# Four of a visit's eight source one-hots gathered from an identity table in DRAM

## The reference

```python
def gcn_conv(x, W, b, src, dst, n_nodes):
    h = x @ W
    deg = jax.ops.segment_sum(jnp.ones_like(dst, dtype=h.dtype), dst, num_segments=n_nodes)
    dinv = jnp.where(deg > 0, jax.lax.rsqrt(deg), 0.0)
    norm = dinv[src] * dinv[dst]
    msgs = h[src] * norm[:, None]
    out = jax.ops.segment_sum(msgs, dst, num_segments=n_nodes)
    return out + b
...
src, dst = add_self_loops(edge_index, n)
h = gcn_conv(x, W1, b1, src, dst, n)
h = jax.nn.relu(h)
out = gcn_conv(h, W2, b2, src, dst, n)
```

## Time and profile before

| | us |
|---|---|
| median of three runs | 4810.34 |
| lowest and highest | 4807.37, 4814.28 |
| the profiled execution, whole | 4806.03 |
| its span | 4803.5 |
| busy in the span: TensorE, VectorE, ScalarE, GpSimd | 3900.7, 2679.1, 1793.9, 1492.7 |

### The profile page before, as it was taken

One profiled execution on the slowest core, in us unless ns is written; L12 is line 12 of the kernel. 1 busy time (PEld: TensorE's weight loads), 2 busy tenths in 40 slices (PEclk: granted clock), 3 DMA queues, 4 the chain that ended last, 5 costly groups with the idle time before them and its releaser, 6 DMA issues. The chain is left out here.

```text
span 4803.5 us, 77604 instructions
## 1 busy us (share of the span) xinstructions
PE 3900.7 (81%) x19093; PEld 2693.1 (56%) x19094; DVE 2679.1 (56%) x8404; ACT 1793.9 (37%) x4836; POOL 1492.7 (31%) x1513
## 2 busy tenths in 40 slices
PE   6989996599975888885877809859588996599999
PEld 4566664344433466664555504325587776488887
DVE  4489999677785367767777786000897213011010
ACT  0067775377761022221666623001896101111111
POOL 0155553477750155553777700000000000211110
PEclk9999998699997999997999959979899996799999
DMA  3278884388862378775888810180000001634342
GB/s 108 78 253 270 271 268 154 109 273 272 270 205 82 86 257 260 255 257 178 277 262 262 266 42 8 40 309 0 0 0 16 8 24 66 258 116 165 104 156 91
DMA packets 204806, 765.45 MB, mean 159 GB/s; under 512 B 36862, under 2 KB 60270, under 8 KB 204734
## 3 DMA queue, kind: packets, MB, share of 16 engines
q0 software_dynamic: 119328, 566.15, 36.8%
q1 hardware_dynamic: 82334, 194.49, 11.6%
q10 hardware_dynamic: 3072, 3.94, 0.3%
HBM read 838.08 MB, written 26.53 MB: 180 GB/s over the span
## 5 line engine op out<-in xcount | busy, mean ns | idle before, releaser
L689 PE MATMUL l_psZ<-X,ident 128*128 128x396 f32 (+3 forms) x2656 | 811.5, 428 | 0.4 <-issue 0.3
L887 POOL DMA_INDIRECT a_g<-fs,pair_src x664 | 716.5, 1079 | 304.2 <-issue 162.0
L625 POOL DMA_INDIRECT X<-fs,near_src x664 | 627.9, 946 | 481.8 <-DVE l_zr L657 167.1
L963 PE MATMUL a_psO<-a_g,a_sel 128*128 128x396 f32 (+1 forms) x1992 | 726.2, 509 | 43.7 <-DVE a_g L911 31.2
L689 PEld LDWEIGHTS l_psZ<-X,ident 128*128 128x128 f32 x2656 | 498.5, 191 | 189.4 <-issue 5.9
L942 ACT ACTIVATE a_g<-a_g,L 128x99 f32<-128x99 f32 (+1 forms) x1494 | 529.1, 428 | 182.4 <-DMA a_g<-fs,pair_src 169.2
L686 PE MATMUL l_psZ<-fd,l_spread 128*128 x1328 | 449.4, 418 | 150.4 <-DVE l_zr L659 69.2
L963 PEld LDWEIGHTS a_psO<-a_g,a_sel 128*128 128x128 f32 x1992 | 376.2, 195 | 314.8 <-issue 120.4
L919 DVE TENSOR_TENSOR acc<-acc,a_psO 128x386 f32 (+2 forms) x664 | 342.9, 558 | 238.3 <-PE a_psO L963 180.3
L686 PEld LDWEIGHTS l_psZ<-fd,l_spread 128*128 128x128 f32 x1328 | 235.1, 190 | 230.4 <-issue 210.3
L2117 PEld LDWEIGHTS r_psH<-r_rowsT,r_w 128*128 128x128 f32 x2916 | 331.2, 193 | 17.4 <-DMA r_w<-in_L_ffn_w 10.5
(11 more groups left out here) (393 smaller groups left out, 5437.0 us busy)
## 6 DMA issues: line engine op xcount, KB each, us to landing
r_w<-in_L_ffn_w SPq DMA_DIRECT2D x54, 3456.0 KB
l_dsts<-near_rows SPq DMA_DIRECT2D x166, 128.0 KB
hw_w<-in_L_ffn_w SPq DMA_DIRECT2D x8, 2304.0 KB
disp<-in_L_ffn_w SPq DMA_DIRECT2D x8, 2304.0 KB
X<-fs,near_src POOLq DMA_INDIRECT x664
a_g<-fs,pair_src POOLq DMA_INDIRECT x664
H<-in_L_ffn_b SPq DMA_DIRECT2D x27, 384.0 KB
X<-in_x SPq DMA_DIRECT2D x2, 3456.0 KB
```

Of the source, the lines that this page charges most:

```text
L625: nc.gpsimd.indirect_dma_start(out=g[:, n % RING, :], out_offset=None, in_=fs, in_offset=bass.IndirectOffsetOnAxis(ap=R.near_src[:, n:n + ...
L689: last = nc.tensor.matmul(psZ[k][:, a, 0:hi - lo], R.ident[:], g[:, j, lo:hi], start=False, stop=True, skip_group_check=True)
L887: nc.gpsimd.indirect_dma_start(out=g[:, n % RING, 0:width], out_offset=None, in_=table, in_offset=bass.IndirectOffsetOnAxis(ap=R.pair_src[ ...
L963: last = nc.tensor.matmul(psO[j][:, a, 0:hi - lo], sel[:, j, k, :].bitcast(F32), g[:, j * 2 + k, lo:hi], start=(k == 0), stop=(k == 1))
```

## The change

`setup` makes an identity table `eye` of 1280 rows by 1280 columns in bfloat16 in DRAM. VectorE clears a strip of 128 by 2432, ScalarE puts the 128 by 128 identity into it and issues ten transfers of 128 rows, each a window of the strip that is shifted by a block; ScalarE waits for the source list before it issues them and for all ten at the end. The same one-hot products that list the sources of the pairs also list the sources of the last four tiles of each visit: `R.wide_src`, 196 columns of indices, by eight small VectorE instructions, eight matmuls and two copies.

In `edge_counts` GpSimd issues 196 gathers, four per visit, each of 128 rows of `eye` with 2560 bytes, into a buffer `fetched` that holds four visits; from the fifth visit on it waits for the matmuls of the visit four before. VectorE makes three source one-hots per visit instead of six and ScalarE one instead of two. TensorE also waits for the gathered rows of the visit; its loop now holds four visits instead of two.

`R.high` is now allocated after `edge_counts`, so its cast moves from `norm_counted` to `gcn_layers`: ScalarE casts a block of H and then copies that block of the counts. VectorE's `low` of a block waits for the cast. In `norm_counted` ScalarE zeroes seven blocks before the square root and three behind it.

```diff
+FETCHED, FETCHES = 4, 4
...
+        @block.scalar
+        def _(act):
+            act.wait_ge(s_strip, 1)
+            act.wait_ge(s_id, 1)
+            nc.scalar.copy(strip[:, ROWS - P:ROWS], R.ident[:]).then_inc(s_strip, 1)
+            act.wait_ge(s_strip, 2)
+            act.wait_ge(s_src, 48)
+            for b in range(NB):
+                act.dma_start(R.eye[b * P:(b + 1) * P, :], strip[:, (NB - 1 - b) * P:(NB - 1 - b) * P + ROWS]).then_inc(s_eye, 16)
+            act.wait_ge(s_eye, 16 * NB)
...
+            nc.vector.memset(strip[:], 0.0).then_inc(s_strip, 1)
...
+            for k in range(FETCHED):
+                last = nc.vector.tensor_scalar(wide_tile[:, k, :], wide_u, float(WIDE), float(WIDE - FETCHED + k), ALU.mult, ALU.add)
+            chain(last)
+            for q in range(4):
+                last = nc.vector.tensor_scalar(wide_hot[:, q], wide_tile[0:TQ], tile_nof[:, q:q + 1], None, ALU.is_equal)
+            last.then_inc(s_hot, 1)
...
+            for h, k0, k1 in ((0, 0, 2), (1, 2, FETCHED)):
+                nc.vector.tensor_copy(R.wide_src[:, k0 * WIDE_VISITS:k1 * WIDE_VISITS], fetched[h])
...
+            pe.wait_ge(s_hot, 3)
+            for h, k0, k1 in ((0, 0, 2), (1, 2, FETCHED)):
+                for q in range(4):
+                    nc.tensor.matmul(fetched[h], rowsf[:, 0, q, :], wide_hot[:, q, k0:k1].rearrange("t k v -> t (k v)"), start=(q == 0), stop=(q == 3))
...
-            for b in range(NB // 2):
+            for b in range(NB - 3):
                 empty(b)
             square_roots(nc, act, W, W.val, W.root)
-            for b in range(NB):
-                act.wait_ge(s_row, b + 1)
-                nc.scalar.copy(R.high[:, b, :], R.H[:, b, :])
-            for b in range(NB // 2, NB):
+            for b in range(NB - 3, NB):
                 empty(b)
...
-    BY_ACT = 2
+    BY_ACT = 1
+    MADE = WIDE - FETCHED
...
-        pick = c.sb("pick", [P, 2, WIDE, ROWS], BF16)
+        pick = c.sb("pick", [P, 2, MADE, ROWS], BF16)
+        fetched = c.sb("fetched", [P, FETCHES, FETCHED, ROWS], BF16)
...
+            for v in range(WIDE_VISITS):
+                if v >= FETCHES:
+                    pool.wait_ge(s_mm, v - FETCHES + 1 + 2)
+                for k in range(FETCHED):
+                    nc.gpsimd.indirect_dma_start(
+                        out=fetched[:, v % FETCHES, k, :], out_offset=None, in_=R.eye,
+                        in_offset=bass.IndirectOffsetOnAxis(ap=R.wide_src[:, k * WIDE_VISITS + v:k * WIDE_VISITS + v + 1], axis=0)).then_inc(s_fetched[v % FETCHES], 16)
...
-                for k in range(WIDE - BY_ACT):
+                for k in range(MADE - BY_ACT):
...
-            def multiply(i, s):
-                v = i * 2 + s
+            def multiply(i, f):
+                v, s = i * FETCHES + f, f % 2
...
+                pe.wait_ge(s_fetched[f], i * 16 * FETCHED + 16 * FETCHED)
                 for b in range(NB):
                     for k in range(WIDE):
-                        last = nc.tensor.matmul(psC[s][:, b * P:(b + 1) * P], pick[:, s, k, b * P:(b + 1) * P], sel[:, s, k, :],
-                                                start=(k == 0), stop=(k == WIDE - 1))
+                        own = pick[:, s, k, b * P:(b + 1) * P] if k < MADE else fetched[:, f, k - MADE, b * P:(b + 1) * P]
+                        last = nc.tensor.matmul(psC[s][:, b * P:(b + 1) * P], own, sel[:, s, k, :], start=(k == 0), stop=(k == WIDE - 1))
...
             for b in range(NB):
+                nc.scalar.copy(R.high[:, b, :], R.H[:, b, :]).then_inc(s_high, 1)
                 nc.scalar.activation(counts[:, b, :], R.CT[:, b, :], ACT.Copy, accum_out=degree[:, b:b + 1]).then_inc(s_count, 1)
...
             for b in range(NB):
+                dve.wait_ge(s_high, b + 1)
                 low_part(b, R.H)
```

More of the change, by code:

```diff
@@ L1435, in edge_counts @@
         away = c.sb("away", [P, BY_ACT, ROWS], F16)
-        pick = c.sb("pick", [P, 2, WIDE, ROWS], BF16)
+        pick = c.sb("pick", [P, 2, MADE, ROWS], BF16)
+        fetched = c.sb("fetched", [P, FETCHES, FETCHED, ROWS], BF16)
+        s_fetched = [c.sem(f"fetched{f}") for f in range(FETCHES)]
         sel = c.sb("sel", [P, 2, WIDE, P], BF16)
@@ L1471, in make @@
                     act.wait_ge(s_away, v * BY_ACT + n + 1)
-                    last = nc.scalar.activation(pick[:, s, WIDE - BY_ACT + n, :], away[:, n, :], ACT.Relu, scale=-1.0, bias=one[:])
+                    last = nc.scalar.activation(pick[:, s, MADE - BY_ACT + n, :], away[:, n, :], ACT.Relu, scale=-1.0, bias=one[:])
                 last.then_inc(s_pick, 1)
@@ L1528, in multiply @@
                 pe.wait_ge(s_pick, v + 2)
+                pe.wait_ge(s_fetched[f], i * 16 * FETCHED + 16 * FETCHED)
                 for b in range(NB):
                     for k in range(WIDE):
-                        last = nc.tensor.matmul(psC[s][:, b * P:(b + 1) * P], pick[:, s, k, b * P:(b + 1) * P], sel[:, s, k, :],
-                                                start=(k == 0), stop=(k == WIDE - 1))
+                        own = pick[:, s, k, b * P:(b + 1) * P] if k < MADE else fetched[:, f, k - MADE, b * P:(b + 1) * P]
+                        last = nc.tensor.matmul(psC[s][:, b * P:(b + 1) * P], own, sel[:, s, k, :], start=(k == 0), stop=(k == WIDE - 1))
                 last.then_inc(s_mm, 1)
-            visits(pe, multiply)
+            with pe.Fori(0, WIDE_VISITS // FETCHES) as i:
+                for f in range(FETCHES):
+                    multiply(i, f)
+            for f in range(WIDE_VISITS % FETCHES):
+                multiply(WIDE_VISITS // FETCHES, f)
 def gcn_layers(nc, R, name, layers):
@@ L2144, in program @@
         R.X = sb("X", [P, NB, D])
-        h_at = nc.sbuf_base
+        h_at = -(-nc.sbuf_base // 32) * 32
         R.H = sb("H", [P, NB, D])
```

17 lines of the change are left out of this document (11 added, 6 removed).

## The result

The changed kernel takes 4874.88 us (median of four runs, 4869.28 to 4877.04) against 4811.51 for the kernel before (4807.37 to 4814.28): 1.0128 times as long, with a 95% interval of 1.0116 to 1.0141. That is **+63 us**, where +20.5 was forecast and the range ended at +42.

The account below looks back on a forecast made before the run. In `edge_counts` three engines were within a microsecond, VectorE's one-hots last; the change would make GpSimd's gathers the bound. 26.5 - 10.0 + 0.8 + 3.2 = +20.5 us, giving 4831 us; range 4796 to 4852.

Parts of the forecast that it names:

- `setup`: Setup stage: +3.2 us, TensorE last there with eight more products and two copies; lists and table transfers hidden.
- `norm_counted`: Normalization stage: 10.0 us earlier, as the casts leave and two zeroings move ahead; VectorE then last.
- `edge_counts`: Edge count stage: +26.5 us, GpSimd's four gathers and their delays making a visit 6.1 us, 0.5 more than before.
- `gcn_layers`: Graph layers: +0.8 us, TensorE starting behind one returned cast; flags some 20 us in, without cover up to 3 more.
- under the source one-hots: Edge counts: gathers starting beside VectorE's source one-hots wait, 0.5 us a visit, the middle between 0 and 0.9.
- 6.1: Edge counts: us per visit, from 5.0 for four gathers, 0.6 under `sel` and 0.5 under the source one-hots.
- only `sel` holds them up: Rival, edge counts: gathers delayed by `sel` alone, 5.5 to 5.6 us a visit, total 4801 to 4806; chance 0.16.
- The other half of the same step: Edge counts: one-hots wait for gathers in turn, 0.2 us up to some 0.6, some of 0.7 us or more.
- Wrong in kind would be a stage in which GpSimd waits for TensorE: Sign, edge counts: GpSimd waiting for TensorE (the buffer) would show the forecast wrong in kind; no size given.

Follow-up runs that it names:

- A: Occasions (chips 4, 3 and 0, and the first measurement) on which the kernel before took 4813.42, 4810.97 and 4807.68 us, as in the first measurement.
- B: Two occasions (chips 2 and 5) on which the kernel before took 4578.14 and 4576.11 us.
- a1: The changed kernel itself, run again in B; 0.9978 of the kernel before.
- n1: The change with VectorE's `sel` run only twice at the start of the stage (counts left out); 1.0134 of the kernel before, in A.
- f3: The change with three gathers a visit instead of four, VectorE making four source one-hots and ScalarE one; 0.995 of the kernel before, in B.
- e3: The kernel before with TensorE's loop in the edge counts over four visits instead of two, nothing else; ratio 1.0, in B.
- r2: The change with TensorE multiplying its own one-hots and SyncE's plain transfers of fixed rows in place of gathers; 0.9926 of the kernel before, in A.
- q1: The change with TensorE multiplying its own one-hots and each gather fetching rows of 32 partitions instead of 128; 1.0123 of the kernel before, in A.
- g1: The change with TensorE multiplying its own one-hots instead of the fetched rows, which still arrive and are waited for; 1.0114 of the kernel before, in A.
- g2: The change with TensorE multiplying its own one-hots and gathers of 128 bytes a row instead of 2560; 1.0109 of the kernel before, in A.
- r1: The change with TensorE multiplying its own one-hots and GpSimd writing numbers in place of each gather, nothing transferred; 0.9979 of the kernel before, in A.

## Why the prediction was wrong

By the budget of the two profiled executions, in us:

| | forecast | measured | rows |
|---|---|---|---|
| `setup` | +3.2 | +3.5 | VectorE's copy at 35.51, now 38.97 |
| attention layers | 0 | +11.0 | from there to the first row of H, 3373.00, now 3387.45 |
| `norm_counted` | -10.0 | -10.0 | H to the numbers: 3373.00 to 3389.90, now 3387.45 to 3394.31 |
| `edge_counts` | +26.5 | +65.6 | numbers to end: 3389.90 to 3673.58, now 3394.31 to 3743.58 |
| `gcn_layers` | +0.8 | about +1 | first `low` 0.9 us behind the last addition, now 1.8 |

The terms but two hold. **`setup`** is right to 0.3 us: TensorE, not the lists of VectorE or the table's transfers, was last. **`norm_counted`** is right: ScalarE's diagonal now ends at 3391.74 and VectorE's last row of H at 3393.44, so VectorE is last, as said. **`gcn_layers`**: the flags come at 3764.53, 20.9 us into it, as said, and they cost TensorE at most a gap of 0.44 us. **The attention layers** should not have moved. They are the same code in the other ten runs of A, which have the table too. From the start of the first normalization to that of `norm_counted` these took 3320.0 to 3332.5 us (3325.9 in the mean), before 3322.6, the change 3333.3. So most of the 11 us is the scatter of the gathering layers between executions; an effect of the table of some 3 us isn't excluded. The medians differ by 63, not 71.

**`edge_counts`** is where it failed, twice and in opposite directions.

*The term "under the source one-hots", 0.5 us a visit, and with it 6.1.* In B, without pauses, all the delay of gathers is 4 x (1.088 - 0.95) = 0.55 us a visit where 0.6 + 0.5 was taken. The visit is 5.57: the rival "only `sel` holds them up" (5.5 to 5.6). Sorting the 196 gathers of a1 by what VectorE did when they started shows that its mechanism is right, too. The 46 that started under `sel` last 1528 ns in the mean, the 53 that started under a source one-hot 960 and the others 946: 0.54 us a visit for `sel`, as forecast, and 0.01 for the one-hots instead of 0.5. The visit shown above has both kinds: the gather of 3552.99 ends 0.81 us behind `sel`, and that of 3554.78, started under the one-hots of 3553.57, lasts 0.95. A one-hot can hold a gather up, but by little: without `sel` (n1) the 48 gathers that started under one have 1030 ns, and with four one-hots a visit (f3) the 26 such gathers have 1077, the longest 1322. One row each way was too little to take the middle of a range. The other half of the same step was right: one-hots are stretched by gathers, 547 to 627 ns, but VectorE had the room. With 5.57 instead of 6.1 the sum is 4810.3 + 20.5 - 49 x 0.53 = 4805, 0.9989 of before; in B the change measured 0.9978.

*What the sum lacked altogether.* TensorE was entered with 4.64 us of matmuls that nothing but a wait can stretch. In A it takes 6.8 beside four gathers, without waiting for anything that the profile names. No rival had this. 47 visits of 5.55 that become 6.76 are +57 us. The first visit, from 3403.73 on, takes 15.6 us instead of 6.8, which adds 8.8: together that is the stage's +65.6. In it TensorE had its longest pauses. Busy for 3.87 of the 10 us from 3410 on, it also had the lower clock for part of them (0.60 in the mean):

```profile
3410.00:3420.00 10.00, 3.87 (x31) 2.87 (x30) 0.27 (x1) 0.27 (x1) 4.87 (x6) 0.60 0.72 222
```

The step that failed is thus the visit itself: its length was taken from GpSimd's gathers, with TensorE's 4.64 us under them. "Wrong in kind would be a stage in which GpSimd waits for TensorE" was the sentence that came true: GpSimd waits 80.5 us for TensorE.

The trace of before had a sign of this, in a view that wasn't read. TensorE's waits in the first `logits`, 245 to 790 us, of the kernel before in A, and then those of e3 in B, 245 to 750:

```profile
PE l_psZ L686 <- issue: 32.7, 22, 24.2
PE l_psZ L686 <- ACT l_spread L602: 14.3, 27, 0.8
```
```profile
PE l_psZ L686 <- ACT l_spread L602: 24.0, 1, 24.0
PE l_psZ L689 <- DMA X<-fs,near_src: 0.9, 1, 0.9
```

The longest wait is the start of the stage in both. What is left is 32.7 - 24.2 = 8.5 us in 21 pauses in A, where gathers run beside TensorE, and none in B. All 21 stand at L686, the first matmuls of a visit, right behind waits of the program; so it isn't shown that they are the same pauses as in `edge_counts`. What is shown is that all the gathering stages are slower in A. From the first to the last gather the two `logits` and two `aggregate` last 540.5, 496.9, 550.5 and 495.8 us in the trace of before and 501.9, 458.9, 449.1 and 447.8 in that of e3. These differences make 226 of the 232 us between the two spans; how much of them TensorE's pauses are isn't known. In the first `logits` it does 3.6 matmuls a microsecond (1976 in 545 us), where a visit of 80 in 4.4 us asks for 18. The gathers' cost was looked for on VectorE alone, because a rule says where to look. The Trainium skill ("SBUF — State Buffer", section "Who interferes with whom") states that TensorE and ScalarE never wait on anyone and that a DMA doesn't contend with a compute engine. For ScalarE (1362 ns against 1354) and for the plain transfers of r2 the traces agree. For TensorE beside gathers in A they don't: 72.1 us in 185 pauses. Of ports the rule may still be true, since q1, g1 and g2 show that it isn't the data that are in the way.

What stays open is what "issue" hides. That the supply of instructions runs dry is argued from the regular 0.73 us, the full pace ahead of the first pause, and the count of gathers. The queues that the profile calls instruction queues don't show it; the page of after has

```profile
q8 instruction: 36, 0.59, 0.1%
q14 instruction: 38, 0.31, 0.0%
```

over the whole span, against 35 and 37 before, far fewer than the 185 pauses. And why A has pauses and B none isn't shown by any run. A gather of `logits` lasts GpSimd the same in both (946 ns in before and in e3), and matmuls do, too (445 ns at L689); the packets of GpSimd's queue took 237 ns in A and 230 in B.

## What to carry to other kernels

Where TensorE runs many short matmuls, count the gathers that GpSimd issues beside it per stretch of matmuls, and look first for idle time of TensorE put down to issue in stages that gather already. That nothing an engine waits for comes late doesn't mean that it keeps its own pace. A result from one chip on one occasion may not hold on another: the same change measured 1.0128 in A and 0.9978 in B. Two gathers a visit instead of four were faster than before in A (0.9947), where four were slower; in r2 plain transfers of fixed rows cost neither TensorE nor VectorE anything.

## What the runs showed of the hardware

- Beside GpSimd's gathers TensorE's short matmuls paused, 2 us a visit, on some occasions (chips 4 and 3) and not on others (2 and 5). Where they did, a visit took 6.75 to 7.17 us with four gathers, 5.8 with three and 4.9 with two; four gathers of 32 rows (6.75) or of 128 bytes a row (6.83) did as much as four of 128 rows of 2560 bytes.
- GpSimd writing numbers for 1.02 us, four times a visit, stretched VectorE's one-hots from 547 to 785 ns, and gathers of 1.04 us only to 627. The Trainium skill ("SBUF — State Buffer", section "Who interferes with whom") states that a VectorE instruction in a two-port mode and a GpSimd instruction exclude each other for their whole length; r1 agrees with it, with 2.82 us for three one-hots in one visit instead of 1.47, and with 1149 ns instead of 978 for the 52 writings that started under a one-hot. The 53 gathers of a1 that started under a one-hot were hardly held up: 960 ns instead of 946.
- A gather of 32 rows isn't much cheaper for GpSimd than one of 128: 862 and 946 ns where nothing delays them (medians of q1 and g1). The means in the stage, 1039 and 1044, are alike because the 47 that started under `sel` last 1558 and 1347 ns.
- With TensorE busy 0.77 of a stretch (g1: 147.03 of 190 us) the granted clock was 1.00, the upper of its two levels. In g2 and n1, with much the same busy time, it fell to the lower level now and then: 0.95 and 0.94 in the mean of the same stretch, 0.83 from 3460 to 3470 us in g2.
